# Cross-attention pair: PV matmuls of score tiles 3, 4 and 5 moved behind the row scores of heads 1, 2 and 3

## The reference

```
q = x @ Wq;  k, v = text @ Wk, text @ Wv;  k_ip, v_ip = ip @ Wk_ip, ip @ Wv_ip
out = softmax(q k^T * s) @ v + softmax(q k_ip^T * s (+ 0.5*sem in layer 1)) @ v_ip (* mask in layer 1)
x = out @ Wo + bo + x
```

## Time and profile before

| | before |
|---|---|
| median of 3 runs | 1900.07 us |
| the profiled execution, its own time | 1900.69 us |
| its span | 1898.9 us |
| TensorE busy (matmul) | 1824.5 us, 96% |
| VectorE busy | 1166.1 us, 61% |
| ScalarE busy | 780.5 us, 41% |
| GpSimd busy | 431.9 us, 23% |
| mean granted TensorE clock | 0.994 |

### The profile page before, as it was taken

The page is one execution under the profiler, slowest core; times in us unless marked ns, Lnnn a source line. Parts: engine busy times, 40 slices in busy tenths (PEclk is TensorE's granted clock), DMA queues, the critical chain, the costliest instruction groups (busy, mean ns, idle before and its releaser), DMA issues.

```text
span 1898.9 us, 53980 instructions
## 1 busy us (share of the span) xinstructions
PE 1824.5 (96%) x23163; PEld 1462.0 (77%) x23163; DVE 1166.1 (61%) x2905; ACT 780.5 (41%) x1569; POOL 431.9 (23%) x520
## 2 busy tenths in 40 slices
PE   7889999999999999998998999999999999999998
PEld 4567888888888888884576788878787888888884
DVE  5776676767676767555543556566665656565653
ACT  3243454454454545443122334434343434343441
POOL 3032332423332424211000112211111112121120
PEclk9999999999999999999999999999999999999999
DMA  6652343443433433424175122323131413232221
GB/s 264 136 174 64 135 139 115 135 131 105 124 118 113 127 119 109 146 81 168 42 126 183 26 55 80 97 70 103 47 114 42 127 50 101 62 110 60 81 57 44
DMA packets 122311, 198.49 MB, mean 105 GB/s; under 512 B 40424, under 2 KB 109432, under 8 KB 115480
## 3 DMA queue, kind: packets, MB, share of 16 engines
q1 hardware_dynamic: 116600, 164.50, 30.7%
q10 hardware_dynamic: 5472, 30.54, 4.3%
HBM read 133.91 MB, written 60.88 MB: 103 GB/s over the span
## 4 chain that ended last, share of the span: by engine, by line
PE 80%; DVE 8%; DMA 5%; ACT 3%; issue 2%; POOL 2%; SPq 0%; ACTq 0%; DVEq 0%
PE proj L512 53%; PE pv L665 5%; PE proj L478 5%; PE rows L618 4%; PE st L641 4%; PE rows L512 3%; PE st L649 2%; DMA arena<-k_dram 2%; DMA k_dram<-arena 2%; PE rows L619 2%; DVE wparts L1354 1%; DMA cbuf<-w_dram 1%; DVE arena L1376 1%; POOL arena L1267 1%; PE rows L627 1%
## 5 line engine op out<-in xcount | busy, mean ns | idle before, releaser
L512 PE MATMUL proj<-w_hl,cbuf 128*128 128x128 f16 x9600 | 603.2, 219 | 0.7 <-issue 0.7
L512 PE MATMUL proj<-cbuf,w_hl 128*128 128x322 f16 (+1 forms) x3840 | 591.5, 300 | 2.2 <-issue 2.2
L512 PEld LDWEIGHTS proj<-w_hl,cbuf 128*128 128x128 f16 x9600 | 553.4, 98 | 12.5 <-issue 1.3
L512 PEld LDWEIGHTS proj<-cbuf,w_hl 128*128 128x128 f16 x3840 | 367.5, 97 | 166.0 <-issue 3.0
L1267 POOL TENSOR_TENSOR arena<-arena 128x400 f16<-128x400 f32 x240 | 235.2, 980 | 932.1 <-ACT arena L1015 932.1
L1014 ACT ACTIVATE arena<-st,rs 128x400 f16<-128x400 f32 x480 | 287.3, 599 | 323.0 <-PE st L649 128.8
L990 ACT ACTIVATE arena<-proj 128x323 f16<-128x323 f32 (+1 forms) x160 | 70.6, 442 | 542.2 <-PE proj L512 530.8
L1015 ACT ACTIVATE arena<-st,rs 128x400 f32<-128x400 f32 x480 | 286.0, 596 | 0.0
L1562 DVE TENSOR_TENSOR arena<-arena 128x400 f16<-128x400 f32 x240 | 144.6, 602 | 146.6 <-ACT arena L1015 143.3
L665 PEld LDWEIGHTS pv<-arena 128*128 128x128 f16 x4480 | 183.4, 97 | 29.5 <-POOL arena L1267 8.2
L665 PE MATMUL pv<-arena 128*128 128x66 f16 (+1 forms) x4480 | 198.2, 185 | 6.9 <-POOL arena L1267 5.7
(11 more groups left out here) (166 smaller groups left out, 1792.5 us busy)
## 6 DMA issues: line engine op xcount, KB each, us to landing
arena<-k_dram SPq DMA_DIRECT2D x240, 185.2 KB, 3.6
k_dram<-arena SPq DMA_DIRECT2D x80, 322.5 KB, 2.9
c_dram<-cbuf SPq DMA_DIRECT2D x16, 1290.0 KB, 6.4
raw<-ctx_dram SPq DMA_DIRECT2D x14, 1290.0 KB, 7.8
cbuf<-c_dram SPq DMA_DIRECT2D x12, 1290.0 KB
cbuf<-w_dram ACTq DMA_DIRECT2D x24, 640.0 KB, 7.5
arena<-q_dram SPq DMA_DIRECT2D x48, 125.0 KB, 2.6
cbuf<-c_dram ACTq DMA_DIRECT2D x2, 2580.0 KB
```

The costliest lines, as they stand in the source:

```text
L512: mm = nc.tensor.matmul(out, x[a](k), w[b](k), start=(k == 0 and m == 0), stop=(k == KT - 1 and m == 2))
```

## The change

In the tail of TensorE's window the three calls `weigh(u, 3)`, `weigh(u, 4)` and `weigh(u, 5)` trade places with `max_scores(n, 1)`, `max_scores(n, 2)` and `max_scores(n, 3)`, which stood right behind them. Nothing is added or removed, and the queues of the other engines are the same.

```diff
                     k_part(k, 0, 2, 5)
                 else:
                     out_tile(l, 0, 0)
+                max_scores(n, 1)
                 weigh(u, 3)
-                max_scores(n, 1)
                 if more2:
                     k_part(k, 0, 5, KT), k_part(k, 1, 0, 1)
+                max_scores(n, 2)
                 weigh(u, 4)
-                max_scores(n, 2)
                 if more2:
                     k_part(k, 1, 1, 4)
                 else:
                     out_tile(l, 0, 1)
+                max_scores(n, 3)
                 weigh(u, 5)
-                max_scores(n, 3)
                 if more2:
                     k_part(k, 1, 4, KT)
                 max_turn(n)
```

## The result

The changed kernel takes 1910.61 us in the median of seven runs (1908.32 to 1916.19), the kernel before 1900.46 us beside it (1896.8 to 1904.18). The ratio is 1.0059, with a 95% interval from 1.0047 to 1.0072, so the change costs 11.2 us, between 8.9 and 13.7. The forecast was 1914.0 us in a range of 1909 to 1918.6, from a sum of 13.7 us. The direction, the place and the mechanism are as forecast. The forecast size is at the upper end of the measured interval.

The account below looks back on a forecast made before the run. TensorE, busy 96% of the span, was taken as the bound. 14.1 − 0.45 = 13.7 us on the profiled 1900.69 us gave 1914.4 us; with the median 0.6 us lower, 1914.0 us, range 1909 to 1918.6 us.

Parts of the forecast that it names:

- Head 1 and tile 3: At head 1, VectorE's release stays put, so the moved PV block costs its full 0.226 us in 62 windows.
- The windows with slack: At head 1 in 7 windows of layer 1 and 6 of layer 0, VectorE is free early: no cost.
- The wait of PV for GpSimd: At tile 3, 5.7 us of waits for L1267 only change name; counted as nothing, at most 5.7 us gained.
- Heads 2 and 3: With tiles 4 and 5 moved, both heads keep their distances, head 3 just in time: 0, at most 4.6 us lost.
- The turn: Behind head 3, tile 5 adds 0.226 us cover, gaining at most 0.01 us a window, 0.8 us in all.
- The second rival: At the turn, tile 5 covers 0.19 us of weight-load waiting per window; 14.8 us return, 1899 us; chance 0.04 alone.
- The last but one windows: In each layer's last but one window, tile 5 falls into the turn's wait, giving back 2 x 0.226 = 0.45 us.
- The sum: Over the whole kernel, 14.1 − 0.45 = 13.7 us more, forecast as 1914.0 us.
- The price per block by page and by row: For a PV block of 8 matmuls, the row gives 0.22 to 0.23 us, the page 0.65 us; row kept.

Follow-up runs that it names:

- Experiment 1: Only PV of tile 3 moved behind head 1, tiles 4 and 5 left in place; against the kernel before: ratio 1.0072, +13.7 us.
- experiment 3: The changed kernel with VectorE's `v_unit(n, 1)` behind `maxima(n, 0)` instead of ahead of it; ratio 0.9951 to the kernel before, −9.3 us.
- experiment 5: The changed kernel with PV of tile 2 also moved, from ahead of head 0 to behind head 1; ratio 1.0130 to the kernel before, +24.7 us.
- experiments 8 and 9: Both kernels again, unchanged, for second traces: the change at ratio 1.0061 (+11.6 us), the kernel before at 1893.43 us in one run.
- Experiment 2: Only PV of tiles 4 and 5 moved behind heads 2 and 3, tile 3 left in place; against the kernel before: ratio 0.9992, −1.5 us.

## Why the prediction was right, and where its size was off

**Head 1 and tile 3, 0.226 us in 62 windows: right.** Head 1 starts the same 1.93 to 1.94 us after head 0, and the PV block costs its full length behind it. The wait before it grows from 0.15 to 0.37 us (716.84 + 1.24 to 718.45), of which the profile's list shows 0.21, for the modelled end of the nine projections covers the rest. Head 1 waits for VectorE in 65 windows in the first trace of the change and in 61 in the second. Experiment 1 puts the price in this one exchange, experiment 3 takes it away by a change on VectorE alone, and experiment 5 doubles it.

**The windows with slack: right for layer 1.** Behind `text_ip`, head 1 comes 1.56 us after head 0, where it came 1.78 (1443.59 to 1445.37), and the window costs 20.24 us as against 20.25. The 38 windows of layer 1 take 784.4 us instead of 778.4, and 784.4 instead of 778.3 in the second pair of traces: 6.0 and 6.1 us, which is 30 windows of 0.20. For layer 0 I had fixed 6 windows by the DMA waits of one trace. Which windows those are is chance, as experiments 8 and 9 show. Layer 0's 38 windows cost 4.6 us more in the first pair of traces and 6.4 us in the second.

**The wait of PV for GpSimd: right.** It left the list but for one wait of 1.0 us outside these windows, and nothing came of it: in a window that splits context head 1 is still 2.81 us behind head 0 (189.88 to 192.69), now with a wait for L1542.

**Heads 2 and 3: right, by a hair.** Head 3 keeps its 1.77 to 1.78 us in all full windows. Experiment 2, where head 2 comes sooner, shows how near it was: there 7 windows lose 0.07 us at head 3. `maxima(n, 2)` ends at 721.48 + 0.82 = 722.30, and head 3 starts 0.13 us later. I had forecast 0.07. VectorE starts 0.67 us after head 2 (at 721.33), where I had counted 0.74.

**The turn: mis-sized, it gives a little back.** I took 0 for it, with a bound of 0.01 us a window. The weight load's wait, 19.5 us in the earlier trace rows, fell to 5.0 us, and experiments 1 and 2 both show what that brings, tile 5 behind head 3 against tile 5 ahead of it: 0.01 us a window in layer 0 and 0.02 us in layer 1, some 1.3 us over 76. The turn now starts 0.27 us after L1550 ends, instead of 0.06 in the earlier trace rows, so it had been only just in time. So 14.5 us less waiting of the load was worth 1.3 us: that a load costs nothing while the array still streams is nearly, not wholly, right. The second rival had the right sign and about a tenth of the size that I gave it (0.19 us).

**The last but one windows: less than I gave them.** I had 0.226 us for each, from tile 5 falling into the wait of the turn. That wait did shrink by 0.21 us. The last but one window of layer 1, where both traces have the full clock, the kernel before in its second trace and the change in its first:

```profile
1842.64 0.38 PE L618 MATMUL rows<-arena 96*128 96x512 f16 x1
...
1855.83 0.35 PE L627 MATMUL rows<-ident,mxh 100*128 100x100 f16 x4 [1.50 <-DVE mxh L1550]
```

```profile
1859.28 0.38 PE L618 MATMUL rows<-arena 96*128 96x512 f16 x1
...
1872.33 0.35 PE L627 MATMUL rows<-ident,mxh 100*128 100x100 f16 x4 [1.29 <-DVE mxh L1550]
```

From head 0 to the turn it is 13.19 us before and 13.05 us after, 0.14 us less. Head 1 comes 0.22 us sooner, as tile 3 no longer stands ahead of it, but from head 2 to head 3, where `out_tile` now runs straight into the row scores, it is 3.99 us instead of 3.92. Layer 0's window can't tell, since its distance from head 0 to the turn moves by more than that from trace to trace: 11.36 to 12.85 us in three traces with the order of before, 11.22 to 12.46 us in five with the changed one. If it gave back as much, the two make 0.3 us instead of 0.45.

**The sum.** With these two terms at what was measured it is 14.1 − 1.3 − 0.3 = 12.5 us. The ratio gives 11.2 and 11.6 us, and the 76 full windows cost 10.6 us more in the first pair of traces and 12.5 us in the second. The rest is less than the intervals, and no run divides it further.

**The price per block by page and by row: the row.** By the 81 ns of the Trainium skill's page "TensorE: Matmul & The Clock Gate", section "Back-to-back issue gap", the estimate was 40 us. The change cost 11.2 us, and a block of 8 takes 0.22 us in the changed kernel too (718.78, and 719.00 for the next projection). The page's figure is for 128 moving columns, and the matmuls of a PV block move 66 and 34 in turn, so it was not made for them. But this kernel's stream of 128 columns does not bear it out either: 24 matmuls at full clock take 1.34 us from the first to the next instruction's start (1053.89 to 1055.23 in the second trace of the kernel before), 56 ns each.

## What to carry to other kernels

Where a TensorE order hands one buffer back and forth with a slower engine, work ahead of the next use is free only as long as it fills the time that engine needs, so measure that time from start to start before moving anything out of it. A wait of 0.15 us in some 48 windows showed in no list of waits, for the modelled end of the matmul ahead covered it, and removing it, with a part of the longer waits in 14 more, was worth 0.5%. Look first at the other engine's order: one VectorE operation placed behind the reduction that TensorE waits for, instead of ahead of it, gained nearly as much as the change lost.

## What the runs showed of the hardware that was not expected

Two traces of the unchanged kernel differ by 7.3 us in span (1898.9 and 1891.6), more than half of what was to be measured. Most of it, 4.4 us, lies at two places where the first trace had the lower clock. The first place is the first window of layer 1. Columns as in the earlier trace rows, first the kernel before in its first trace, then in its second, the same stretch of time, in which the second trace is 2.7 us further on in the program:

```profile
1050.00:1065.00 15.00, 11.99 (x148) 10.60 (x146) 8.40 (x28) 3.14 (x7) 0.36 (x1) 0.77 0.01 1
```

```profile
1050.00:1065.00 15.00, 11.99 (x201) 10.53 (x200) 8.96 (x28) 6.64 (x14) 1.90 (x2) 1.00 0.01 1
```

In the first trace TensorE had waited 1.51 and 1.50 us with one row-score block between, and the next 24 matmuls took 2.76 us. In the second it had waited twice 1.50 us at the same instructions, and the 24 matmuls took 1.50 us. First trace, then second:

```profile
1054.43 0.39 PE L618 MATMUL rows<-arena 96*128 96x512 f16 x1 [1.51 <-DVE mx L1538]
...
1056.73 2.76 PE L512 MATMUL proj<-w_hl,cbuf 128*128 128x128 f16 x24
```

```profile
1051.71 0.39 PE L618 MATMUL rows<-arena 96*128 96x512 f16 x1 [1.50 <-DVE mx L1538]
...
1053.89 1.50 PE L512 MATMUL proj<-w_hl,cbuf 128*128 128x128 f16 x24
```

The matmuls of the first are nearly twice as long, which is the step between the clock's levels of 1.2 and 2.4 GHz. The first window of layer 1 took 20.67 us in the one and 17.99 in the other. Over the traces of all kernels here it took 17.99 or 18.00 us in seven and 19.05 to 20.82 us in four. The second place is the last but one window of layer 1, behind a wait of 1.6 us for L1527. First trace, then second:

```profile
1850.27 5.29 PE L478 MATMUL proj<-qo,cbuf 128*128 128x400 f32 x10 [1.60 <-DVE arena L1527]
```

```profile
1844.71 3.60 PE L478 MATMUL proj<-qo,cbuf 128*128 128x400 f32 x10 [1.59 <-DVE arena L1527]
```

The same idle time may or may not be followed by the lower clock, and each time it was, it cost 1.1 to 2.8 us here. Single traces of two kernels are best compared window by window, where the clock is 1.00 in both, and not by their spans.
